# Softplus as one activation, a bf16 time-step projection and unrolled images in a fused convolution and Mamba kernel

## What is computed

```python
dbl = u @ x_proj_w.T                       # 8 + 16 + 16 rows: step input, B, C
dt  = softplus(dbl[:, :8] @ dt_proj_w.T + dt_proj_b)
h_t = exp(dt_t * A_n) * h_(t-1) + (dt_t * u_t) * B_(t,n)     # per state n
y_t = sum over n of h_(t,n) * C_(t,n)
```

## Time and profile before

| | |
|---|---|
| median of 3 runs | 14,233.76 us (14,220.4 to 14,238.92) |
| span of the profiled execution | 14,223.5 us |
| instructions recorded | 202,410 |
| busy: POOL | 13,343.7 us, 94% |
| busy: DVE | 12,957.9 us, 91% |
| busy: PE | 12,521.2 us, 88% |
| busy: ACT | 10,502.8 us, 74% |
| DMA, mean share of 16 engines | some 60%, 220 GB/s |

### The profile page before, as it was taken

One profiled execution on the slowest core, in us unless ns is written; L12 is line 12 of the kernel. 1 busy time (PEld: TensorE's weight loads), 2 busy tenths in 40 slices (PEclk: granted clock), 3 DMA queues, 4 the chain that ended last, 5 costly groups with the idle time before them and its releaser, 6 DMA issues.

```text
span 14223.5 us, 202410 instructions
## 1 busy us (share of the span) xinstructions
PE 12521.2 (88%) x64412; PEld 7971.6 (56%) x64412; DVE 12957.9 (91%) x8813; ACT 10502.8 (74%) x14525; POOL 13343.7 (94%) x4106
## 2 busy tenths in 40 slices
PE   7888888899888888888988888888888888888886
PEld 4555555555555555555555555555555555555554
DVE  7999999999999999999999999999999999999986
ACT  5777777777777777777777777777777777777764
POOL 7999999999999999999999999999999999999985
PEclk8999999999999999999999999999999999999997
DMA  5666556655556566566655665665656656666553
GB/s 194 229 227 225 223 218 225 230 220 221 224 222 231 222 223 226 219 231 226 222 221 221 224 227 221 223 224 221 231 222 225 223 221 226 230 221 225 222 207 121
DMA packets 564038, 3134.39 MB, mean 220 GB/s; under 512 B 63826, under 2 KB 63834, under 8 KB 300642
## 3 DMA queue, kind: packets, MB, share of 16 engines
q1 hardware_dynamic: 562914, 3120.59, 59.0%
HBM read 3057.42 MB, written 46.14 MB: 218 GB/s over the span
## 4 chain that ended last, share of the span: by engine, by line
POOL 46%; issue 33%; PE 9%; DVE 7%; ACT 3%; DMA 1%; POOLq 1%; DVEq 0%; SPq 0%; ACTq 0%
POOL ring L977 27%; POOL ring L960 17%; PE work L1478 5%; DVE ring L1466 4%; DVE slot L1452 2%; PE y_acc L1493 2%; ACT L994 1%; POOL yz L927 1%; PE slot L1478 1%; ACT ring L1170 1%; DMA b_rows<-cb_rows_scratch 1%; ACT u_conv L1033 0%; PE slot L1493 0%; PE y_acc L1478 0%; PE work L1493 0%
## 5 line engine op out<-in xcount | busy, mean ns | idle before, releaser
L977 POOL TENSOR_TENSOR ring<-ring,c_rows 128x2048 f32<-128x2048 f32 x2048 | 9290.7, 4543 | 481.7 <-DVE ring L1466 472.0
L1466 DVE TENSOR_TENSOR_SCAN ring<-ring,slot 128x1024 f32<-128x1024 f32 x2432 | 5544.8, 2284 | 327.5 <-PE slot L1493 58.2
L1493 PE MATMUL y_acc<-wk,ring 128*128 128x128 f32 x32768 | 4455.2, 284 | 474.9 <-POOL ring L977 393.6
L1493 PEld LDWEIGHTS y_acc<-wk,ring 128*128 128x128 f32 x32768 | 3950.2, 147 | 1519.4 <-POOL ring L977 691.7
L960 POOL TENSOR_TENSOR ring<-du,b_rows 128x1024 f32<-128x1024 f32 x1664 | 3944.6, 2372 | 71.1 <-DVE du L1277 55.0
L1466 DVE TENSOR_TENSOR_SCAN ring<-slot,ring 128x1024 f32<-128x1024 f32 x1664 | 3783.3, 2274 | 184.4 <-POOL ring L960 115.3
L1452 DVE TENSOR_TENSOR slot<-du,slot 128x1024 f32<-128x1024 f32 x2240 | 2714.1, 1212 | 163.7 <-PE slot L1478 123.2
L1170 ACT ACTIVATE slot<-dt,a_neg 128x1024 f32<-128x1024 f32 x1664 | 1855.8, 1115 | 1338.0 <-DVE ring L1466 1322.5
L1170 ACT ACTIVATE ring<-dt,a_neg 128x1024 f32<-128x1024 f32 x2432 | 2737.4, 1140 | 123.2 <-PE y_acc L1493 66.3
L1478 PE MATMUL slot<-stack,sel 96*128 96x512 bf16 x4480 | 1422.8, 401 | 687.6 <-DVE ring L1466 648.0
L1478 PE MATMUL work<-h_new,fused 128*128 128x512 f32 x4096 | 1977.9, 613 | 25.5 <-ACT yz L1082 19.3
(11 more groups left out here) (182 smaller groups left out, 11461.3 us busy)
## 6 DMA issues: line engine op xcount, KB each, us to landing
c_rows<-cb_rows_scratch SPq DMA_DIRECT2D x2048, 1024.0 KB, 4.7
b_rows<-cb_rows_scratch SPq DMA_DIRECT2D x1664, 512.0 KB, 5.5
x_next<-in_x SPq DMA_DIRECT2D x32, 512.0 KB, 6.5
x_new_scratch<-x_next SPq DMA_DIRECT2D x32, 512.0 KB, 7.3
h_old<-h_new SPq DMA_DIRECT2D x32, 512.0 KB, 2.9
x_old<-x_new_scratch SPq DMA_DIRECT2D x32, 512.0 KB, 6.5
out<-x_old SPq DMA_DIRECT2D x32, 512.0 KB, 5.7
cb_rows_scratch<-stack SPq DMA_DIRECT2D x128, 96.0 KB
```

The source lines that it names most:

```text
L977: pool.tensor_tensor(pair, pair, c_rows[:, k % CB_BUFS, :, :], ALU.mult).then_inc(prod_ready, 1)
L1466: dve.tensor_tensor_scan(slot, a, b, 0.0, MUL, ADD).then_inc(scan_done, 1)
L1493: ins = pe.matmul(chunk(out_t, j), chunk(x, j), kc("ident"), is_transpose=True, start=start and j % (BANK // P) == 0, stop=stop, skip_grou ...
```

## The change

- The time step's softplus is one activation, `dt_soft`, in place in PSUM. It has an activation table of its own (`softplus`); the table `HOME` is now `exp_and_others`, which has exp and tanh. The five steps `dt_abs`, `dt_relu`, `dt_exp`, `dt_ln` and `dt_add` are gone, and `dtsoft2` takes the place of five steps in layer 3.
- `dt_proj` is one bf16 matmul of 96 rows on `stack`. The x projection puts its 8 step rows into the three bf16 parts, beside B, and `dtw3` holds the weights split into three bf16 parts; six new steps `dtw` on DVE, nine small instructions in all, make them once at the start.
- `KINDS` has 66 units of kind D, 51 of P and 11 of Z. Every pass now has at least one unit of kind Z, so `turn_du` runs for all 8 passes (it ran for 4), and `z_t` has two buffers.
- `each_image` has no loop: 32 images stand one after the other in each engine's program, and each wait is on a constant.
- The wait for the last use of `du` moves from ACT's `dt_abs` to DVE's `dt_u`. Some holds between streams change.
- `SHIFTS` has new numbers throughout. `PACE` is the same.

```diff
-KINDS = ('DPDPDPDDDPDPDPDP', 'DPDPDPDDDPDPDPDP', 'DDDDDPZPDPDDZPDP', 'DPDPDPDPZPDPDPDP',
-         'DPDPDPDPDPDPDPDP', 'DPDPDPDDDPDPDPDP', 'DPDPDDDPDZDDDPDP', 'DPDPDZDPDDDZDPDP')
+KINDS = ('DDPPDPDPDPDZDDDP', 'DPDPDPDDDZDPDPDP', 'DDDDDPZPDPDDPPDP', 'DPDPDPDPZPDPPDDP',
+         'DDZPDPDPDPDPDPZP', 'DPDDPPDZDPDPDPDP', 'DPDZDDZPDPDDDPDP', 'DPDPDZDPDPDZDPDP')
+Z_BUFS = 2
-HOME = "natural_log_exp_and_others"
-TABLE = {**dict.fromkeys(("silu", "silu2", "gate_tanh", "xa_tanh", "sine", "q_sin"), "silu_and_others"),
+HOME = "exp_and_others"
+TABLE = {**dict.fromkeys(("silu", "silu2", "sine", "q_sin"), "silu_and_others"),
          **dict.fromkeys(("squeeze_gelu", "mlp_gelu"), "gelu_and_others"),
-         **dict.fromkeys(("decay", "dt_exp", "dt_ln", "dtexp2", "dtln2", "decay2", "a_exp", "a_exp2"), HOME)}
+         **dict.fromkeys(("dt_soft", "dtsoft2"), "softplus"),
+         **dict.fromkeys(("decay", "decay2", "a_exp", "a_exp2", "gate_tanh", "xa_tanh"), HOME)}
@@ timestep
-        rows = [("dt_cb_rows", d, c)] if (d, h) != (0, 1) else []
-        steps += [step(("dt_proj", d, h, c), "P", b, rows)]
-        steps += [step((k, d, h, c), e, b) for k, e in (("dt_abs", "A"), ("dt_relu", "A"), ("dt_exp", "A"), ("dt_ln", "A"),
-                                                        ("dt_add", "P"), ("dt_copy", "A"), ("dt_u", "D"))]
+        parts = [("part", d, 2, c)] if (d, h) != (0, 1) else []
+        steps += [step(("dt_proj", d, h, c), "P", b, parts)]
+        steps += [step((k, d, h, c), e, b) for k, e in (("dt_soft", "A"), ("dt_copy", "A"), ("dt_u", "D"))]
@@ each_image
-            body("first", 0)
-            if images > 2:
-                turns = next(k for k in (3, 2, 1) if (images - 2) % k == 0)
-                with eng.Fori(0, (images - 2) // turns) as t:
-                    for i in range(turns):
-                        body("mid", t * turns + 1 + i)
-            if images > 1:
-                body("last", images - 1)
+            for s in range(images):
+                body("first" if s == 0 else "last" if s == images - 1 else "mid", s)
@@ ACT
+                elif k == "dt_soft":
+                    ins = act.activation(w, w, ACT.Softplus, bias=kc("dt_b", name[2], name[2] + 1))
+                elif k == "dt_copy":
                     _, d, h, c = name
+                    used = d * 2 * NST + (h - 1) * NST
+                    if s * UNITS + used > 0:
+                        act.wait_ge(decay_ready, s * UNITS + used)
+                    ins = act.activation(half(dt[:, h, :], c), w, ACT.Copy)
@@ DVE
                 elif k == "dt_u":
                     _, d, h, c = name
+                    used = d * 2 * NST + (h - 1) * NST
+                    if s * UNITS + used > 0:
+                        dve.wait_ge(input_ready, s * N_D + number("D", used))
+                        dve.wait_ge(pool_input, s * N_P + number("P", used))
@@ PE
                 elif k == "dt_proj":
                     _, d, h, c = name
-                    ins = mm(w, dtw_sb[DTP:DTP + RANK, h * P:(h + 1) * P], half(dt_rows, c), True, True)
-                elif k == "dt_add":
-                    _, d, h, c = name
-                    ins = mm(w, kc("ident"), half(du[:, h, :], c), False, True)
+                    ins = mm(w, dtw3[0:96, h * P:(h + 1) * P], half(stack[0:96, d % 2, :], c), True, True)
@@ PE turn_z
-                    turn(operand[u % 2], z_t[:, :], True, True).then_inc(z_turned, 1)
+                    turn(operand[u % 2], z_t[:, (s * N_Z + number("Z", u)) % Z_BUFS, :], True, True).then_inc(z_turned, 1)
```

More of the change, by code:

```diff
@@ L256, in set_up @@
     weights += [step(("diag", h), "D") for h in range(HALVES)]
+    weights += [step(("dtw", i), "D") for i in range(2 * PARTS)]
     decays = [step(("a_exp",), "A"), step(("a_exp2",), "A"), step(("a_neg",), "D"), step(("a_neg2",), "D")]
@@ L352, in first_of, with last_z @@
     return u % NST == KINDS[u // NST].index(kind)
-def last_z(u):
-    return max([v for v in range(u) if kind_of(v) == "Z"], default=None)
+def last_z(u, back=1):
+    return ([None] * back + [v for v in range(u) if kind_of(v) == "Z"])[-back]
 def unit_programs(kind):
@@ L435, in deadlines, with wanted @@
     return until
-def lay(streams, kind, pace, soon_within=SOON, shifts=()):
-    programs = unit_programs(kind) if kind in ("first", "mid", "last") else dict.fromkeys("PADG", [])
+def wanted(streams, pace, shifts=()):
     by = {("result", 1): 2 * OUT_AT - 8, ("dt_u", 0, 0, 1): UNITS - 4, ("part", 0, 2, 1): UNITS - 2}
@@ L464, in lay @@
             want[x[0]] += .5 * more
+    return want
+def lay(streams, kind, pace, soon_within=SOON, shifts=()):
+    programs = unit_programs(kind) if kind in ("first", "mid", "last") else dict.fromkeys("PADG", [])
+    want = wanted(streams, pace, shifts)
     free, at = dict(LAG if kind in ("mid", "last") else dict.fromkeys("PADG", 0.)), dict.fromkeys("PADG", 0)
@@ L560, in finish_plan, with image_streams @@
     return best_plan([mix() + back(), decays], "finish", PACES)
-def image_plan(first, last):
-    kind = "first" if first else "last" if last else "mid"
+def image_streams(first, last):
     def pass_end(d, h):
@@ L805, in hold @@
                     for other in "ADG":
-                        if not (isinstance(base[other], int) and base[other] == 0):
+                        if base[other] > 0:
                             need[other] = max(need.get(other, 0), 0)
@@ L1023, in step @@
                     _, src, dst = NORM[name[1]]
-                    if name[1] == "1" and not (isinstance(s, int) and s == 0):
+                    if name[1] == "1" and s > 0:
                         act.wait_ge(h_kept, 16 * s)
@@ L1441, in side_steps @@
                         hold(dve, "D", base, of, after)
-                        step(name, s + 1 if name in ahead else s, bank_of[bank])
+                        step(name, s + 1 if name in ahead or name[:3] == ("dt_u", 0, 0) else s, bank_of[bank])
                 for u in range(UNITS):
```

151 lines of the change are left out of this document (71 added, 80 removed), and 61 rows, old and new, of the table SHIFTS.

## The result

| | before | after |
|---|---|---|
| median of the timed runs (us) | 14,229.7 (14,220.4 to 14,238.9, 4 runs) | 14,109.0 (14,104.0 to 14,111.8, 4 runs) |
| ratio, 95% interval | | 0.991 (0.9896 to 0.9924) |
| span of the profiled execution (us) | 14,223.5 | 14,102.1 |
| mean granted TensorE clock | 0.946 | 0.920 |
| period of an image, mean of the 30 intervals between output transfers (us) | 437.9 | 434.0 |

The change gains 0.9%, 121 us, where I had forecast 2.4%. The time lies in the range and beside the rival "DVE's relief isn't passed on" (14,120 us).

What follows compares the result with a forecast made beforehand. The prediction took DVE with its gaps as the bound, POOL right behind. Its terms took an image from 436.7 to 425.8 us: -327 us for thirty images, -10 us for the ends, giving 13,890 us, range 13,700 to 14,120.

Steps and rivals of the forecast that it cites:

- DVE's relief isn't passed on: Rival: DVE, now early, waits for POOL's inputs instead; 433 us an image, about 14,120 us; chance 0.15.
- The register instructions and the loop edge: On DVE, gaps before scans fall from 7.8 to 2.4 us an image (-5.4); turn ends go (-1.4).
- DVE's savings count nearly in full: Claim that DVE's savings reach the period, since the forecast 425.8 us an image stays above POOL's 420.5 us.
- POOL's floor: Least time an image needs on POOL: 423 us before, about 420.5 us with one input less.
- Fewer units of kind D and P: DVE loses four multiplies, -4.8 us an image, all on the path; POOL loses one input, -2.4 us.
- PE's relief: PE gives back 24.5 us an image; DVE's waits for PE shrink, ends 0 and -4 us, taken as -1.0.
- Softplus on ACT: One activation replaces four per time step, with 28 new table loads an image; ACT at 354.4 us, not the bound.
- The +1.2 us for the blocks: Latency of softplus blocks on ACT, 3.2 us each that no decay can enter: ends 0 and +2.7 us an image.
- the slower rival: Rival: softplus blocks on ACT hold up decays; 439.1 us an image, about 14,300 us; chance 0.07.
- Z units' turns, moved wait, start: Waits for turned Z +0.5 us an image; moved wait on DVE 0; `dtw` steps at the start 0 to 3 us in all.
- Order: New order may shift POOL's waits in layer 3 or make another step late: ends -4 and +4 us, value 0.
- First and last image, and ends: First and last image gain from the kinds only, the ends a little from shorter chains: -10 us in all.

Runs made afterwards that it cites:

- b_unroll: The kernel before with its loop written out as 32 images and nothing else changed: 14,136.3 us, ratio 0.9921.
- a_zd: The kernel after with its seven new Z units put back to kind D (multiply on DVE): 14,273.1 us, ratio 1.0019.
- b_noadd: b_unroll with the fp32 addition of each time step on PE left out: 14,290.1 us, ratio 1.0036.
- a_noload: The kernel after with relu in place of softplus and no table loads for it: 14,105.5 us, ratio 0.9899.
- b_soft: b_unroll with the time step's softplus as one activation and no addition on PE: 14,387.1 us, ratio 1.0097.
- b_soft_noload: b_soft with relu in place of softplus and no table loads for it: 14,271.9 us, ratio 1.0020.

## Why the prediction was wrong, point by point

**The register instructions and the loop edge: the size of the gaps right, what they are worth wrong.** I had 5.4 + 1.4 = 6.8 us in an image. The unnamed idle time fell to (10.6 - 3.8 - 0.6) / 3 = 2.1 us (forecast 2.4), and DVE's groups show no idle time that ends with "issue" in the stretch, where the earlier trace rows have 3.4 us. Of the 6.8 us the period got 3.1 (b_unroll). The step that failed is the sentence that DVE's savings count nearly in full because the sum stays above POOL's floor. A floor made of busy times says only that POOL isn't the limit by its sum; it counts neither a pass that ends with a serial chain through PE, DVE and POOL, nor the results of PE for which DVE then waits: in b_unroll these waits grew from 13.0 to 17.6 us in an image. That the steady part of after is no faster than that of b_unroll (433.5 and 433.6 us) shows how little of the rest of the change reached the time there.

**Fewer units of kind D and P.** -4.8 us on DVE. Seven units were passed on by 0.65 (a_zd), which for four gives some -3 us, an estimate from that run.

**PE's relief: the sign was wrong.** I took -1.0 us from ends of 0 and -4, and had no end above nothing, without a reason that excludes one. This is the second step that failed. b_noadd measures +5.2 us for the addition alone, in the order of before. Nor did PE get 24.5 us freer: in the three images it is busy for 1,163.42 - 1,137.51 = 25.9 us less, 8.6 in an image, and over the whole run 411.7 / 32 = 12.9, since what is left on it runs at the lower clock more of the time. The earlier trace rows show the clock, 0.96 and 0.91, and I read past them: with less PE work the clock fell, and the chain that ends the fourth pass paid for it. There was a reading miss as well: I counted 7.2 us of DVE's waits for PE in an image, from the three groups of the earlier trace rows, where all its groups give 13.0; among those not counted was L1318, the last link ahead of the reduction, with 6.8 us in three images, which became 18.4.

**Softplus on ACT: right, and its latency cheaper than feared in the new order.** 0.661 us (forecast 0.656), 60 loads in an image (62), ACT at 1048.9 / 3 = 349.6 us (354.4), 81% of the period. DVE's waits for ACT are 1.7 us in an image, below the 5 that I had set as the test. I had read 2.7 us for them before, from three rows; all groups give 4.8. The +1.2 us for the blocks doesn't show in the new order (a_noload) and is 3.8 in the old one (b_soft against b_soft_noload), so the slower rival has its mechanism there, at about a quarter of its price.

**Z units' turns, moved wait, start.** DVE's waits for turned Z fell from 5.4 to 3.8 us in the stretch, so +0.5 was about 0. The moved wait has no row of its own in DVE's groups, as forecast.

**Order.** I gave it 0, within 4 us. The parts that were measured, each in one order only: -3.1 (loop), +5.2 (addition off PE), some -3 (kinds), 0 (loads): -0.9 us; the whole change gives -3.9, of which 0.8 is the last interval's share (3.2 us come in the others). The missing 3 us lie in the last image's plan, the new order and the bf16 projection together, which weren't parted by a run; and by the steps of the period such parts need not add up.

**First and last image, and ends.** I had -10 us for them. The first transfer comes 6.4 us earlier and the last interval is 23.8 us shorter (3.3 of them in b_unroll too, 469.0 us). That the error of the whole isn't larger is owed to this; in the steady part 3.2 of 10.9 us came.

**The tests I had set.** "POOL's waits for scans stay at 13 us though DVE is lighter" is what came, in a variant: 11.2 us for scans and 8.0 us, up from 4.1, for the chain in layer 3. POOL's idle time, which I had at 10 us or less, is (1,310 - 1,251.8) / 3 = 19.4. The rival "DVE's relief isn't passed on" gave the time, 14,120 against 14,109 us (its own terms, -3.8 x 30 - 10, add up to 14,110). That it came so near is luck: its period was 433 us by POOL's 2.4 us and the loop edges, while the register instructions did bring something, the relief of PE cost, and 24 us came with the last image. Its mechanism holds in a small part: DVE's waits for POOL's inputs grew from 10.8 to 17.4 us in three images, 2.2 in an image, but those for PE by 10.0 in an image.

## What to carry to other kernels

Before pricing a saving on the busiest engine, find the serial chain that ends each stage, and see which engine runs its links; the saving counts only in stages that such a chain doesn't end. Price relief of PE with both signs: look at the granted clock of the stage, at the durations that the same matmul has in this trace at either level, and at who waits for them; here 19 us less PE work cost 5 us. Where PE's links are on the chain, make them fewer or cheaper, which gave 1% here, rather than fill PE with work to hold its clock. And look at the period of single images, not at their mean alone: images that all take the same time, in kernels with different work, say that something else holds them.

## What the runs showed of the hardware

In the order of before, a matmul that does nothing useful raised the granted clock from 0.914 (b_soft) to 0.942 with 128 rows, and left it at 0.913 with 8 rows, though the first takes 0.644 us and the 8-row matmuls of that run 0.674 us on average. A table load takes 1.283 us of ACT and no more: in the timeline of after one starts at 5038.15, the softplus behind it at 5039.44, and the next load at 5040.75, right behind the copy that follows the softplus (and in three images 180 loads have 3.2 us of idle time ahead of them in all):

```profile
5038.15 1.28 ACT L998 ACT_TABLE_LOAD   x1
5039.44 0.66 ACT L1050 ACTIVATE work<-work,wk 128x512 f32<-128x512 f32 x1
5040.13 0.60 ACT L1056 ACTIVATE dt<-work 128x512 f32<-128x512 f32 x1
5040.75 1.28 ACT L998 ACT_TABLE_LOAD   x1
```

The Trainium skill, "ScalarE: Activation LUTs", section "What ACT_TABLE_LOAD costs", has about 1.38 us of drain on top; these rows don't agree with that. Straight code of this length streams, as the Trainium skill, "Runtime: NRT & Kernel Launch", section "Instruction fetch mechanics", has it: with all 32 images written out, DVE's waits in the stretch name no "issue" at all.
